# Feed-forward stage of a decoder kernel: rounding, copy of the turned tile, down projection and final add in another order

## The reference, cut to what matters

```python
def _L0_ffn_ref(x, gate_w, gate_b, val_w, val_b, out_w, out_b):
    def bit_linear(x, w, b):
        gamma_x = jnp.clip(jnp.max(jnp.abs(x), axis=-1, keepdims=True), 1e-05, None)
        scale_x = 127.0 / gamma_x
        x_dq = jnp.clip(jnp.round(x * scale_x), -128.0, 127.0) / scale_x
        ...
        gamma_w = jnp.clip(jnp.mean(jnp.abs(w)), 1e-05, None)
        w_dq = jnp.clip(jnp.round(w / gamma_w), -1.0, 1.0) * gamma_w
        ...
        return jnp.einsum('bsd,hd->bsh', x_ste, w_ste) + b
    gate = jax.nn.silu(bit_linear(x, gate_w, gate_b))
    val = bit_linear(x, val_w, val_b)
    return bit_linear(gate * val, out_w, out_b)
...
x = x + _L0_ffn_ref(_layernorm(x, axis=-1), ...)
```

## Time and profile before

| | us |
|---|---|
| median of 3 runs | 1356.46 |
| lowest, highest of them | 1351.54, 1356.58 |
| the profiled execution | 1355.58 |
| its span, first to last instruction | 1353.8 |
| feed-forward stage in it, first to last rounding of a hidden tile (L1241) | 133.19 to 230.94 |

### The profile page before, as it was taken

How to read it: one execution, slowest core, us unless ns; L and a number is a source line. 1 busy time by engine, 2 the same in 40 slices (tenths; PEclk the granted TensorE clock), 3 DMA queues, 4 the chain that set the end, 5 groups by cost and what they waited for, 6 DMA issues and landing times.

```text
span 1353.8 us, 22120 instructions
## 1 busy us (share of the span) xinstructions
PE 1112.8 (82%) x6352; PEld 725.6 (54%) x6353; DVE 864.4 (64%) x2396; ACT 628.9 (46%) x1971; POOL 318.5 (24%) x465
## 2 busy tenths in 40 slices
PE   3676777789898779999999999999999999643690
PEld 2453444566666444556656566565665656432580
DVE  4676575687778747768676686766867776143252
ACT  1435676455555426455454554645546455021230
POOL 1213230132112313223131231322313210013334
PEclk9856999899999889899999999999999999855795
DMA  9401000122111000000000000000000000341454
GB/s 319 149 0 32 0 1 0 48 59 84 46 46 51 13 1 1 1 1 1 1 1 0 1 1 0 0 0 1 1 0 0 0 1 1 101 148 43 129 123 141
DMA packets 42436, 52.42 MB, mean 39 GB/s; under 512 B 4080, under 2 KB 34672, under 8 KB 42096
## 3 DMA queue, kind: packets, MB, share of 16 engines
q1 hardware_dynamic: 36464, 43.11, 10.1%
q10 hardware_dynamic: 4352, 4.20, 1.6%
q0 software_dynamic: 1536, 4.20, 1.0%
HBM read 34.71 MB, written 16.78 MB: 38 GB/s over the span
## 4 chain that ended last, share of the span: by engine, by line
PE 46%; DVE 5%; ACT 4%; issue 3%; DMA 2%; POOL 2%; ACTq 1%; SPq 0%; DVEq 0%; POOLq 0%
PE PS L1481 40%; PE PS L1824 2%; PE PS L1806 2%; DMA rows_dram<-cosT 1%; ACT arena L1345 1%; POOL rows_dram L1116 1%; ACT arena L1354 1%; POOL arena L1131 1%; DVE early L862 1%; DVE arena L686 1%; DVE arena L722 1%; PE PS L1491 1%; DVE arena L710 1%; SPq L942 0%; ACT arena L1465 0%
## 5 line engine op out<-in xcount | busy, mean ns | idle before, releaser
L1481 PE MATMUL PS<-EW,arena 128*64 (+4 forms) x896 | 174.1, 333 | 18.6 <-DVE small L710 9.0
L1481 PEld LDWEIGHTS PS<-EW,arena 128*128 128x128 f32 (+1 forms) x896 | 125.2, 158 | 61.9 <-issue 42.3
L1481 PE MATMUL PS<-early,arena 128*32 128x128 f32 (+6 forms) x864 | 106.8, 358 | 33.4 <-DVE early L573 23.7
L1481 PE MATMUL PS<-wq,EW 128*128 128x512 f32 x256 | 127.2, 620 | 6.8 <-DVE arena L686 6.7
L1080 POOL TENSOR_SCALAR small<-small 128x4 f32<-128x4 f32 x64 | 26.5, 414 | 451.5 <-ACT mask L1338 374.7
L710 DVE CUSTOM_DVE_ANT_0 arena<-PS,kmask 128x128 f32<-128x128 f32 (+3 forms) x256 | 91.6, 383 | 50.2 <-PE PS L1481 45.4
L1354 ACT ACTIVATE arena<-arena,small 128x128 f32<-128x128 f32 (+3 forms) x256 | 119.4, 470 | 0.2
L1481 PE MATMUL PS<-wo,early 128*128 128x256 f32 x512 | 114.8, 382 | 0.8 <-ACT early L1368 0.8
L1345 ACT ACTIVATE arena<-PS 128x512 f32<-128x512 f32 x64 | 38.2, 598 | 160.9 <-PE PS L1806 160.9
L1481 PEld LDWEIGHTS PS<-wo,early 128*128 128x128 f32 x512 | 96.0, 190 | 18.5 <-issue 6.1
L982 POOL TENSOR_SCALAR ve<-mv 128x2 f32<-128x2 f32 x48 | 10.6, 221 | 371.1 <-DVE mv L345 371.0
(11 more groups left out here) (245 smaller groups left out, 2343.5 us busy)
## 6 DMA issues: line engine op xcount, KB each, us to landing
EW<-in_masksT_dram SPq DMA_DIRECT2D x32, 256.0 KB, 3.5
results_dram<-EW SPq DMA_DIRECT2D x32, 128.0 KB, 3.2
EW<-results_dram SPq DMA_DIRECT2D x4, 1024.0 KB, 9.5
rows_dram<-cosT SPq DMA_DIRECT2D x1, 4096.0 KB, 19.6
arena<-rows_dram SPq DMA_DIRECT2D x16, 256.0 KB, 3.2
results_dram<-early ACTq DMA_DIRECT2D x16, 256.0 KB, 3.2
X<-in_x_dram SPq DMA_DIRECT2D x1, 2048.0 KB, 9.0
wq<-in_wq_dram SPq DMA_DIRECT2D x1, 2048.0 KB, 11.2
```

The source lines that it names most:

```text
L1481: return pe.matmul(dst, lhs, rhs, start=first, stop=last)
```

## The change

On ScalarE the copy `evict` of the tile before moves from the head of a step to behind `quantised`, and `levels(b + 1)` moves behind that copy. On TensorE `down` of the tile before moves from between `gate` and `value` to the end of the step, behind `turn`. On VectorE each `narrow` is issued a step later, so that the output step sizes `c_so` need two sets. The level turn of a batch goes into bank 0 and the right half of bank 7 instead of banks 5 and 6; with that `turn(b, 0)` no longer waits for `levels`, while `level_turn` waits for `narrow(b - 1, 0)` (c_y) and `down(b - 1, 1)` for `levels(b + 1)` (s_xt). The rounding of `ew`, the wait for the weights of the self attention and the three constants move from behind the loop to ahead of it. The first projection of the self attention waits for c_y.

```diff
@@ vector engine
-            def narrow(b, j, at=7):
+            def narrow(b, j, par, at=7):
...
-                dve.scalar_tensor_tensor(tokens(b, j), PS[:, at, 0:D], c_so[:, j:j + 1], tokens(b, j), ALU.mult, ALU.add)\
+                dve.scalar_tensor_tensor(tokens(b, j), PS[:, at, 0:D], c_so[:, par, j:j + 1], tokens(b, j), ALU.mult, ALU.add)\
...
-                    if j == 1:
-                        narrow(b, 0)
-                    elif type(b) is not int or b > 0:
-                        narrow(b - 1, 1)
+                    if type(b) is not int or b > 0:
+                        narrow(b - 1, j, 1 - par)
...
             prepare(1, 1)
-            over_parities(dve, ffn)
-            narrow(B - 1, J - 1, 1)
-
             dve.wait_ge(s_l5, 64)
             ternary(ew[:, :, :], ew[:, :, :], 2.0)
             mark["ew"] = count[0]
-
             dve.wait_ge(s_l3, 16 * 7)
+            const(dve.tensor_reduce(d_half, hmask[:, :].rearrange("p (a e) -> p e a", e=2), AX.X, ALU.add))
+            const(dve.tensor_scalar(d_bq, bqk[:, 0:2], 0.25, None, ALU.mult))
+            const(dve.tensor_copy(d_mask, causal[:, 0, 0:P]), "self")
+            over_parities(dve, ffn)
+            narrow(B - 1, 0, 1)
+            narrow(B - 1, 1, 1, 1)
@@ scalar engine, levels and ffn
-                act.activation(cXT.rearrange("p c s -> p (c s)"), bank(5), ACT.Identity, bias=unmagic[:, 0:1])
-                act.activation(cRT, PS[:, 6, 0:S], ACT.Copy).then_inc(s_xt, 1)
+                act.activation(cXT.rearrange("p c s -> p (c s)"), bank(0), ACT.Identity, bias=unmagic[:, 0:1])
+                act.activation(cRT, PS[:, 7, D:D + S], ACT.Copy).then_inc(s_xt, 1)
...
                 for j in range(J):
-                    if j == 1:
-                        evict(b, 0)
-                    elif type(b) is not int or b > 0:
-                        evict(b - 1, 1)
                     if j == 0 and left > 0:
                         rounded(b + 1)
                     if j == 0:
                         gated(b, 1, par)
                     elif left > 0:
                         gated(b + 1, 0, 1 - par)
-                    if j == 0 and left > 0:
-                        levels(b + 1)
                     if j == 1 and left == 2:
                         applied(b + 2)
                     quantised(b, j)
+                    if j == 1:
+                        evict(b, 0)
+                    elif type(b) is not int or b > 0:
+                        evict(b - 1, 1)
+                    if j == 0 and left > 0:
+                        levels(b + 1)
@@ tensor engine
-                after(pe, c_ht, 2 * b - 2)
+                after(pe, c_y, b - 1)
                 for j in range(J):
-                    pe.transpose(PS[:, 6, j * P:(j + 1) * P], cR[:, j, :], ident[:, :])
+                    pe.transpose(PS[:, 7, D + j * P:D + (j + 1) * P], cR[:, j, :], ident[:, :])
...
-            def turn(b, j, mixed):
+            def turn(b, j):
                 u = J * b + j
                 after(pe, c_ht, u)
-                if mixed:
-                    pe.wait_ge(s_xt, FFN * B + b + 2)
...
-            def down(b, j, at=7):
+            def down(b, j, at=7, mixed=False):
                 pe.wait_ge(c_ht, J * b + j + 1)
-                if j == 1:
+                if mixed:
+                    pe.wait_ge(s_xt, FFN * B + b + 3)
+                if at == 7 and j == 1:
                     pe.wait_ge(c_y, b + 1)
...
-                    if j == 1:
-                        down(b, 0)
-                    elif type(b) is not int or b > 0:
-                        down(b - 1, 1)
                     if j == 0:
                         value(b, 1)
                     elif left > 0:
                         value(b + 1, 0)
                     if j == 0 and left > 0:
                         level_turn(b + 1)
-                    turn(b, j, j == 0 and left > 0)
+                    turn(b, j)
+                    if j == 1:
+                        down(b, 0)
+                    elif type(b) is not int or b > 0:
+                        down(b - 1, 1, 7, left > 0)
...
+            pe.wait_ge(c_y, B)
             project(0, 0, d_pq)
```

More of the change, by code:

```diff
@@ L258, in decoder_kernel @@
         cHS = cut(1152, (HID,)); cH = cut(2176, (2, HID)); cHR = cut(4224, (HID,)); cHT = cut(5248, (HC, P), BF)
-        c_gx = small[:, 8:10]; c_sx = small[:, 12:14]; c_hm = small[:, 22:23]; c_sh = small[:, 24:26]; c_so = small[:, 26:28]
+        c_gx = small[:, 8:10]; c_sx = small[:, 12:14]; c_hm = small[:, 22:23]; c_sh = small[:, 24:26]; c_so = small[:, 26:30].rearrange("p (a j) -> p a j", a=2)
         c_neg = small[:, 448:450]; c_off = small[:, 450:452]
@@ L499, in widen, with step_size @@
                     .then_inc(c_h, 1)
-            def step_size(b, j):
+            def step_size(b, j, par):
                 u = J * b + j
@@ L508, in step_size @@
                 dve.wait_ge(c_s, 3 * u + 2)
-                dve.tensor_scalar(c_so[:, j:j + 1], c_hm, gam[:, 2:3], None, ALU.mult)
+                dve.tensor_scalar(c_so[:, par, j:j + 1], c_hm, gam[:, 2:3], None, ALU.mult)
                 dve.reciprocal(c_sh[:, j:j + 1], c_hm).then_inc(c_s, 1)
-            def narrow(b, j, at=7):
+            def narrow(b, j, par, at=7):
                 u = J * b + j
@@ L522, in ffn @@
                     widen(b, j, par)
-                    step_size(b, j)
+                    step_size(b, j, par)
                     if j == 0 and left == 2:
@@ L664, in self_attention @@
                             turn_key(0, k)
-            const(dve.tensor_reduce(d_half, hmask[:, :].rearrange("p (a e) -> p e a", e=2), AX.X, ALU.add))
-            const(dve.tensor_scalar(d_bq, bqk[:, 0:2], 0.25, None, ALU.mult))
-            const(dve.tensor_copy(d_mask, causal[:, 0, 0:P]), "self")
             self_keys(0, 0)
@@ L1504, in level_turn @@
                         at = c * S + j * P
-                        last = pe.transpose(PS[:, 5, at:at + P], cXQ[:, j, c * P:(c + 1) * P], ident[:, :])
+                        last = pe.transpose(PS[:, 0, at:at + P], cXQ[:, j, c * P:(c + 1) * P], ident[:, :])
                 last.then_inc(s_xtp, 1)
@@ L1612, in turn @@
                 last.then_inc(c_t, 1)
-            def down(b, j, at=7):
+            def down(b, j, at=7, mixed=False):
                 pe.wait_ge(c_ht, J * b + j + 1)
-                if j == 1:
+                if mixed:
+                    pe.wait_ge(s_xt, FFN * B + b + 3)
+                if at == 7 and j == 1:
                     pe.wait_ge(c_y, b + 1)
-                elif type(b) is not int or b > 0:
+                elif at == 7 and (type(b) is not int or b > 0):
                     pe.wait_ge(s_x, FFN * B + b)
```

## The result

The changed kernel takes 1373.49 us (median of 6 runs, 1370.59 to 1375.99) against 1356.23 us before. The medians alone stand 1.3% apart; compared over all runs the ratio is 1.0137, with a 95% interval from 1.0114 to 1.016. The prediction was 1361.5 us, at most 1369: the sign was expected, the size wasn't, and the range doesn't hold it.

What follows compares the result with a forecast made beforehand. No engine was full: TensorE and ScalarE took turns, 13.3 us a batch. Terms -1.3 - 0.4 + 3.0 + 2.7 + 1.0 = +5.0 us on the profiled 1355.58 gave 1360.6, forecast as 1361.5 us, range 1354 to 1369.

Steps and rivals of the forecast that it cites:

- The ring: Feed-forward loop: turn, `down`, `gate`, `gated`, rounding and copy in series, 14.04 us a batch against 13.3; chance 0.60.
- The last three tiles: Tiles 12 to 15: 16.5 us against 13.75 before, +2.7 us.
- the seam: From the last rounding to the self attention's first copy: 9.2 us against 8.18, +1.0 us.
- What was said to cost nothing: `level_turn` waiting for VectorE's `narrow`, and the roundings of `ew` and constants ahead of the first `widen`: 0 us.
- the forecast's three terms for it: Tiles 0 to 4, 4 to 12 and 12 to 15: -0.4, +3.0 and +2.7 us.
- the one on the clock: Tiles 0 to 4: as many falls of TensorE's clock after as before, 1.4 us each, within a term of -0.4 us.
- The rival: Loop: TensorE's clock falls in each of seven batches, at most 1.7 us each, +12.7 us, 1369 us; chance 0.22.
- the stretch without a product: TensorE, level turn to next `gate`: 4.12 us once a batch before; 3.05 and 4.0 us after, the longest a little shorter.
- That the clock never falls in the loop: TensorE's bursts spread more evenly, no falls: +0.8 us, 1357.3 us; chance 0.10.
- That no ring closes: Loop: the holes go and each batch takes 9.7 to 10 us, about 1337 us; chance 0.08.

Runs made afterwards that it cites:

- after_products: The changed kernel with idle products in both stretches of a batch where TensorE has no product (five, twelve, eight for batch 6): 1360.81 us, ratio 1.0033.
- after_turns: The changed kernel with 9, 22 and 15 turns of a constant tile in TensorE's two idle stretches of a batch: 1361.57 us, ratio 1.004.
- before_products: The kernel before with eight idle products ahead of the turn of tile (b, 0): 1355.56 us, ratio 1.0001.
- gate_early: The changed kernel with `down` behind the next `gate`, gate of tile (b + 1, 1) ahead of turn (b, 1), final add ahead of statistics on VectorE: 1342.19 us.
- after_copy_first: The changed kernel with ScalarE's order as in the kernel before, all else as changed: 1374.81 us, ratio 1.0126.
- after_products_long: The changed kernel with idle products only in the long stretch ahead of the turn of tile (b, 1): 1359.67 us, ratio 1.0025.
- gate_early_stats: `gate_early` without its edit on VectorE, the final add again behind the statistics: 1341.57 us, ratio 0.9887.
- before_products_late: The kernel before with eight idle products ahead of the turn of tile (b, 0) in batches 1 to 6 only: 1355.3 us, ratio 0.9987.

## Why the prediction was wrong, point by point

**The ring was right.** Its two steps were put at 6.53 and 7.51 us; undisturbed ones measure 6.50 (tiles 12 to 13) and 7.48. The last three tiles without their fall take 16.5 us, as forecast, the seam 9.4 against 9.2. What was said to cost nothing did: `level_turn` doesn't wait for VectorE, and the constants fit into VectorE's idle time.

The total of `after_products`, +4.3 us, looks like the +5.0 forecast, but by luck: the forecast holds three falls in either kernel, the run none in the loop. What isolates the ring is the way from rounding 0 to rounding 15 at the full clock in both orders, `after_turns` and `before_products`:

```profile
132.36 1.24 ACT L1238 ACTIVATE arena<-arena,magic,small 128x1024 f32<-128x1024 f32 x1 [0.40 <-DVE small L510]
...
231.72 1.24 ACT L1238 ACTIVATE arena<-arena,magic,small 128x1024 f32<-128x1024 f32 x1 [1.24 <-DVE small L510]
```
```profile
137.20 1.24 ACT L1241 ACTIVATE arena<-arena,magic,small 128x1024 f32<-128x1024 f32 x1
...
230.58 1.24 ACT L1241 ACTIVATE arena<-arena,magic,small 128x1024 f32<-128x1024 f32 x1 [0.79 <-DVE small L510]
```

That is 99.36 against 93.38 us: the ring costs 6.0 us there, and the forecast's three terms for it were -0.4 + 3.0 + 2.7 = +5.3.

**The step that failed is the one on the clock.** The sum charged the changed kernel "with as many" falls as before, three of 1.4 us. There were seven, together 15.8 us. The rival said "One in each of seven batches" and put it at 1369, with a chance of 0.22. Its count was right, its price not: "A low stretch of 3.4 us holds back at most 1.7 us" took the length from the old rows. In the new order the low clock met a ring in which turn, `down` and `gate` are in series. From the turn's start to `gated` it takes 171.79 - 168.60 = 3.19 us at 2.4 GHz and 182.10 - 176.15 = 5.95 at 1.2 GHz; and in four of seven cases the clock stayed low for 6.8 us, so that all of it ran slow: 2.8 us each and not 1.7. 4 x 2.75 + 3 x 1.65 = 16 us; less the 4.2 already in the forecast and with its 5.0, that makes 16.8 of the 17.3 us measured. A fall that stayed at 3.4 us did cost what the rival said, 1.6 to 1.7.

**Why the chance was too low.** I counted the length of the stretch without a product, 4.12 us before and 4.0 after, and concluded that it was a little shorter. I let the turns in it count for nothing. The Trainium skill ("TensorE: Matmul & The Clock Gate", section "Part 4: PE-mode transpose") says that a turn doesn't count as TensorE being busy in the way a product does. `after_turns` contradicts that here: its float32 turns kept the clock at 1.00 in all of the 98 us. What the runs show to matter is TensorE's idle time. Before, it came in two parts, 2.35 us with a level turn ahead of it, and 1.07. After, the longer part is 3.10 us. The same page's section "HAM oscillation — how this bites in real kernels" describes a loop whose idle gap lets the clock fall in every iteration. The trace agrees: a fall in each of seven batches. For the kernel before I had counted three falls in some eight stretches; it has seven of them.

**The other rivals.** That the clock never falls in the loop came true only where the holes were filled (as in `after_products` and `after_turns`) or shorter (`gate_early`, at most 1.7 us from tile 1 to tile 14). That no ring closes was excluded by the queues, as the prediction's argument said. It became half true only when `gate` and `down` had left the ring.

## What to carry to other kernels

When an instruction is moved behind another on an in-order engine, follow the cycle that closes through the single buffers and add it up on all engines: here a hole of 1.25 us was traded for `down` and `gate` in series, and one more move (`down` behind the next `gate`) was worth 15 us, about half of it through fewer and shorter falls. Look at the holes that the new order leaves TensorE, the longest first; if they grow, price the lower clock over the whole serial piece behind it, in every round, and not by the falls of the old trace. Where such a hole can't be closed, idle products or turns in it are cheap: 12.7 us gained by them here in a kernel that didn't need their results. In the kernel before, with three falls, the medians show no such gain.

## What the runs showed of the hardware

- Float32 turns through the array hold the granted clock at 1.00 as products do: 9 and 22 of them in a batch (`after_turns`), no fall in 98 us.
- In the changed kernel the clock fell once in each of seven batches, in or just behind a hole of 3.03 to 3.10 us (six times) or 2.05 us (once); another hole of 2.05 us, ahead of the turn of tile 14, brought no fall. In the kernel before, holes of 2.27 to 2.35 us, with others of 0.93 to 1.25 us between them, did in three of seven batches. Holes of 2.03 to 2.35 us ahead of both turns of a batch (`after_copy_first`) brought eleven falls, holes of 1.25 to 1.41 us alone (`after_products_long`) none. A hole of 1.67 us ahead of the turn of tile 1 brought a fall in `gate_early_stats`, one of 1.68 us none in `gate_early`. So the longest hole by itself doesn't tell.
- The low stretches at 1.2 GHz inside the loop and at the seam lasted 3.4 or 6.8 us; inside the loop 6.8 us occur in the changed kernel alone. In the kernel before, in the changed one with ScalarE's part undone and in the one with `down` behind the next `gate` all last 3.4 us there.
- The kernel before with idle products was still at 1.2 GHz in the stage's first matmuls up to 135 us (`before_products`) and 134 us (`before_products_late`), the changed kernel up to 134.4 us, the kernel before up to 128.5 us; with the same code ahead of the stage. The first rounding of the two came 3.4 to 4.0 us later than in the kernel before, of which 2.0 to 2.4 us arose ahead of the stage. That is as much as the effect that was to be measured.
